# Conditioned four-layer residual stack on one core: VectorE and GpSimd work of the second layer put in another order

## The chip, the cores and the metric

The kernel runs on 1 core of one Trainium2 chip. The metric is the device time of one execution in microseconds; the time before is 3216.46 us, the median of 3 runs (3215.81 to 3218.46).

## The reference, cut to what matters

x is 32 sequences of 128 tokens with 512 features, in float32. Each layer adds its result to x.

```python
def reference(x, cond, mask, ...):
    x = x + layer0(x, cond)            # attention, modulated
    x = x + layer1(x, mask, cond)      # attention, then RMS norm (below)
    x = x + layer2(x, cond)            # x' = x + attention(norm(x)); x' + swiglu(norm(x'))
    x = x + layer3(x, cond)            # quaternion mix
    return x

def layer1(x, mask, cond):
    q, k, v = heads(x @ Wq.T), heads(x @ Wk.T), heads(x @ Wv.T)     # 16 heads of 32
    scores = where(mask, -inf, q @ k.T * 32 ** -0.5)
    out = merge(softmax(scores) @ v) @ Wo.T
    xn = out / sqrt(mean(out * out, -1) + 1e-6) * rms_scale
    shift, sc = split(silu(cond) @ Wc.T + bc, 2)                    # one pair per sequence
    return xn * (1 + sc) + shift
```

## The kernel before, in words

Activations are kept transposed, features on partitions. The 4096 tokens are cut into `G` = 16 groups of two sequences (`T` = 256 tokens, `CH` = 4 chunks of 128 features). A phase `prepare` is followed by `attention` three times, with the tags L0, L1 and L2, and by `gated_mlp`. The profile's names leave the digit out, so all three attentions read `L_...`. The change touches `attention` alone.

float32 products are made of parts: a tile x is split into a high part `xh` (ScalarE's copy to the matmul's rounded type, `high_x`) and a low part `xl` = x - xh (`low_x`), and each product is three matmuls: high by high, low by high, high by low. So are q, k and the output `ot`; probabilities and values are split in the same manner (`pth`/`ptl`; `v1`, `v2`, `v3` with the remainder `vr` on GpSimd: `rest_of_values` makes `vr`, `third_values` writes `v3`, shown as `keep_v`).

The order is written out by hand, in program order for each engine; semaphores join them. One iteration `body(i)` has `SLOTS` = 12 slots. In slots 0 to 7 TensorE makes the scores of units 0 to 7 of group i (a unit is four heads of one sequence) and, one slot later, transposes the unit's exponentials (L625); later slots hold the products with the values. Between these stand pieces of projections: of the output of group i - 1 in slots 0 and 1 (L574 to L576 with `L_oth`), then K, Q and V of group i + 1. For each unit VectorE takes the maximum (`L_top`, L953) and subtracts it (`L_shifted`, L957), ScalarE takes the exponential (L799), TensorE transposes, ScalarE and VectorE read the two parts (`L_pth`, `L_ptl`). Every two units `normalise(i, j)` on VectorE divides a quarter of the attention's result by the sums (L969 to L984), in slots 4, 6, 8 and 9. `turn_output` transposes it, `low_output` (L998) makes its low part in slots 8 and 11; the output projection waits for the last one.

Layer L1 normalises the projected output `af` of group i - 1 within `body(i)`: in slot 4 VectorE copies gain and shift columns (`norm_gains`) and folds the squares (`add_squares`: `L_half`, then `L_quarter`); in slot 6 TensorE sums over partitions (`norm_sum`, L681, which waits for `L_quarter`) and ScalarE takes the root; in slot 7 VectorE takes the reciprocal (`norm_start`); in slot 9 `norm_scale` (L1021) multiplies `af` by it, after the last `normalise`; in slot 11 `norm_add` adds af times gain to `xres` in eight instructions (L1039) and signals `y_ready`, on which SyncE stores the group. `xres` is x, to which GpSimd has added the shift (`shift_residual`, L1196), as soon as `norm_gains` has signalled. GpSimd's `low_x` (L1154) stands at the end of its body (the first group's is made on VectorE, L1054), and TensorE's first K projection and SyncE's next load of x wait for it (`x_split`).

L2 uses the same functions on the next x (`norm_scale`, and `norm_end` with L1029 in place of `norm_add`), and keeps GpSimd's `low_x`.

Of the kernel before, what the change touches and what calls it, by code (L numbers as in the profile page):

```python
# [51 lines left out]
def f32(ap):  # L52
    return ap.bitcast(F32)
# [292 lines left out]
def attention(nc, hold, k, tag, x_in, x_out, wh, wl, weights):  # L346
# [7 lines left out]
    with ExitStack() as ctx:  # L354
# [66 lines left out]
        sq_ready, sum_step = sem("sq_ready"), sem("sum_step")  # L421
        norm_step, eps_set, y_ready, gains_ready = sem("norm_step"), sem("eps_set"), sem("y_ready"), sem("gains_ready")

# [483 lines left out]
        def _(dve):  # L907
# [98 lines left out]
            def norm_gains(n, gains, biases):  # L1006

                if positive(n):
                    dve.wait_ge(y_ready if L1 else x_normed, n)
                nc.vector.tensor_copy(gt[:], gains[:, :, bass.ds(NB * n, NB)])  # L1010
                nc.vector.tensor_copy(bt[:], biases[:, :, bass.ds(NB * n, NB)]).then_inc(gains_ready, 1)

# [9 lines left out]

            def norm_end(n, tile, out_sem):

                dve.wait_ge(norm_step, 2 * n + 2)
                for c in range(CH):
                    for b in range(NB):
                        part = tile[:, c, b * P:(b + 1) * P]
                        last = nc.vector.tensor_scalar(part, part, gt[:, c, b:b + 1], bt[:, c, b:b + 1], ALU.mult, ALU.add)  # L1029
                last.then_inc(out_sem, 1)  # L1030

            def norm_add(n):

                dve.wait_ge(norm_step, 2 * n + 2)
                dve.wait_ge(res_ready, n + 1)
                for c in range(CH):
                    for b in range(NB):
                        o = slice(b * P, (b + 1) * P)
                        last = nc.vector.scalar_tensor_tensor(out=xres[:, c, o], in0=af[:, c, o], scalar=gt[:, c, b:b + 1], in1=xres[:, c, o],  # L1039
                                                              op0=ALU.mult, op1=ALU.add)  # L1040
                last.then_inc(y_ready, 1)

            if L1 or L2:
                nc.vector.memset(eps[:], 1e-6).then_inc(eps_set, 1)
            if L2:
                add_squares(0)
                ws.low(dve, 0)
                norm_gains(0, k["g1"], k["b1"])
                norm_start(0, 0)
                norm_scale(0, xf)  # L1050
                norm_end(0, xf, x_normed)

            dve.wait_ge(x_high, 1)
            nc.vector.tensor_tensor(xl[:], xf[:], f32(xh[:]), ALU.subtract).then_inc(x_split, 1)  # L1054
            if L2:
# [3 lines left out]
            for s in range(SLOTS):  # L1059
                if s == 6 and L2:  # L1060
                    add_squares(1)
                for n in split_after(s):
                    ws.low(dve, n)
                for fill in ended(s):
                    if active(-1, fill):
                        read_fill(0, fill)
                if s == 7 and L2:
                    norm_gains(1, k["g1"], k["b1"])
                    norm_start(1, 1)
                    norm_scale(1, xf)  # L1070
                    norm_end(1, xf, x_normed)

            def body(i):
                first = isinstance(i, int) and i == 0
                for s in range(SLOTS):
# [6 lines left out]
                    for fill in readable(s):  # L1082
                        if active(i, fill):
                            read_fill(group_of(i, fill), fill)
                    if s in (4, 6, 8, 9):
                        normalise(i, (4, 6, 8, 9).index(s))
                    if 1 <= s <= UNITS:
                        low_probs(i, s - 1)
# [32 lines left out]
                    if s == 4 and L2 and has(i, 2):  # L1121
                        norm_gains(i + 2, k["g1"], k["b1"])
                        add_squares(i + 2)
                    if s == 9 and L1 and not first:
                        norm_scale(i - 1, af)
                    if s == 9 and L2 and has(i, 2):
                        norm_scale(i + 2, xf)
                    if s == 7 and L1 and not first:
                        norm_start(i - 1, b_turn(i, "norm"))
                    if s == 7 and L2 and has(i, 2):  # L1130
                        norm_start(i + 2, b_turn(i, "norm"))
                    if s == 11 and L1 and not first:
                        norm_add(i - 1)
                    if s == 11 and L2 and has(i, 2):
                        norm_end(i + 2, xf, x_normed)
                    if s == 7 and L0 and has(i, 1):
# [6 lines left out]
            if L1:  # L1143
                norm_gains(G - 1, k["gain"], k["shift"])
                add_squares(G - 1)
                norm_start(G - 1, 3 * G - 1)
                norm_scale(G - 1, af)
                norm_add(G - 1)

        @block.gpsimd  # L1150
        def _(pool):
# [27 lines left out]
            def body(i):  # L1179
# [4 lines left out]
                if has(i, 1):  # L1184
                    if L0:
                        low_t(i + 1)
                    for b in range(NB):
                        rest_of_values(i + 1, b)
                if has(i, 2):
                    low_x(i + 2)  # L1190

            def shift_residual(n):
                pool.wait_ge(gains_ready, n + 1)
                pool.wait_ge(res_loaded, 16 * (n + 1))
                x4 = xres[:].rearrange("p c (b t) -> p c b t", b=NB)
                nc.gpsimd.tensor_tensor(x4, x4, bt[:].unsqueeze(3).broadcast_to([P, CH, NB, P]), ALU.add).then_inc(res_ready, 1)  # L1196
# [530 lines left out]
```

## Time and profile before

| | |
|---|---|
| median of 3 runs | 3216.46 us |
| profiled execution, its own time | 3217.66 us |
| its span | 3215.6 us |
| mean granted TensorE clock | 0.968 |
| L0 attention / L1 attention / L2 attention / MLP begin at about | 37 / 779 / 1478 / 2100 us |
| busy share: TensorE, VectorE, ScalarE, GpSimd | 94%, 67%, 43%, 20% |

PE is TensorE, DVE is VectorE, ACT is ScalarE, POOL is GpSimd, SPq the queue of SyncE. A name `L_xres<-L_af,L_gt,L_xres` gives the tile that an instruction writes and those that it reads; `L_bank_...` are PSUM banks, all other tiles of these rows lie in SBUF. In a timeline a row with x8 stands for eight instructions in a row, from the start of the first to the end of the last. The idle time before an instruction counts from the modelled end of the one before it.

### The profile page before, as it was taken

To read this page: it belongs to the slowest core of one execution; us is meant where nothing else is said; L and a number is where in the kernel's file an instruction comes from. 1 tells how busy PE (TensorE), PEld (TensorE's weight loads), DVE (VectorE), ACT (ScalarE), POOL (GpSimd) and SP (SyncE) were. 2 spreads that over 40 slices of the span, in tenths; PEclk is the share of its full clock that TensorE was granted. 3 is DMA by queue.
4 is the path that set the end of the run, shared out by engine and by line. 5 is a ranking of instruction groups with operands and counts; after the bars stand their busy time and mean duration, and the time that the engine had idled before them with its cause. 6 is when DMAs were issued, how large, how long until landed. Compare 5 with 4: busy or idle time off the path is not lost. (4 is left out here: it accounts for less than half of the span.)

```text
span 3215.6 us, 67582 instructions
## 1 busy us (share of the span) xinstructions
PE 3015.6 (94%) x25333; PEld 2713.8 (84%) x25333; DVE 2143.1 (67%) x3771; ACT 1373.5 (43%) x2220; POOL 631.7 (20%) x432
## 2 busy tenths in 40 slices
PE   6999999997899999984999999869999999999998
PEld 5999999996888888884999999858888888888886
DVE  5777677775688888885788888664444454556544
ACT  3444444443455555553566566432222233222221
POOL 1112222110122222211111221112222221111111
PEclk8999999998999999996999999979999999999999
DMA  5444344433444444433455555331122132111111
GB/s 164 113 111 108 101 108 107 110 99 114 112 116 117 115 115 117 115 95 115 122 139 136 130 137 133 98 137 53 66 67 77 53 112 72 53 40 39 52 40 40
DMA packets 198921, 317.07 MB, mean 99 GB/s; under 512 B 42112, under 2 KB 99584, under 8 KB 198304
## 3 DMA queue, kind: packets, MB, share of 16 engines
q1 hardware_dynamic: 198816, 315.64, 35.5%
q8 instruction: 70, 1.15, 0.2%
q14 instruction: 35, 0.29, 0.0%
HBM read 122.53 MB, written 41.94 MB: 51 GB/s over the span
## 5 line engine op out<-in xcount | busy, mean ns | idle before, releaser
L1560 DVE TENSOR_TENSOR mlp_act_t<-mlp_bank_u,mlp_sg 128x512 f32<-128x512 f32 x128 | 88.4, 691 | 452.8 <-ACT mlp_sg L1462 449.2
L799 ACT ACTIVATE L_shifted<-L_shifted,keep_lift 128x512 f32<-128x512 f32 x384 | 275.8, 718 | 190.2 <-DVE L_shifted L957 188.0
L1462 ACT ACTIVATE mlp_sg<-mlp_bank_g 128x512 f32<-128x512 f32 x128 | 76.6, 598 | 627.6 <-PE mlp_bank_u L1375 627.4
L1602 POOL TENSOR_TENSOR mlp_al<-mlp_act_t,mlp_ah 128x512 fp32r<-128x512 f32 x128 | 174.8, 1366 | 856.5 <-ACT mlp_ah L1468 856.5
L953 DVE TENSOR_REDUCE L_top<-L_bank_s 128x4 f32<-128x512 f32 x384 | 262.9, 685 | 111.2 <-PE L_bank_s L616 109.4
L794 ACT ACTIVATE L_pth<-L_bank_t 128x512 f16<-128x512 f32 x384 | 227.7, 593 | 228.3 <-PE L_bank_t L625 227.9
L961 DVE TENSOR_TENSOR L_ptl<-L_bank_t,L_pth 128x512 f16<-128x512 f32 x384 | 262.2, 683 | 79.8 <-ACT L_pth L794 79.0
L1161 POOL TENSOR_TENSOR L_vr<-L_vf,keep_v 128x512 f32<-128x512 f32 x96 | 122.0, 1272 | 884.7 <-ACT keep_v L829 884.7
L625 PE MATMUL L_bank_t<-keep_pack,L_shifted 128*128 128x128 f32 x1536 | 251.9, 288 | 43.3 <-ACT L_shifted L799 43.0
L957 DVE TENSOR_TENSOR L_shifted<-L_bank_s,L_top 128x512 f32<-128x512 f32 x384 | 265.5, 691 | 18.4 <-DVE L_top L953 3.3
L574 PE MATMUL L_bank_a<-L_xh,L_wkh 128*128 128x256 f32 x768 | 231.9, 302 | 38.3 <-DVE L_wkl L102 24.3
L616 PEld LDWEIGHTS L_bank_s<-L_ks,L_qs 96*128 96x128 f32 x1536 | 222.0, 196 | 20.0 <-issue 6.8
L641 PE MATMUL L_bank_o<-keep_v,L_pth 128*128 128x34 bf16 x4608 | 232.8, 179 | 5.3 <-DVE L_of L984 5.2
L574 PE MATMUL L_bank_a<-L_oth,L_woh 128*128 128x256 f32 x768 | 230.1, 300 | 4.5 <-DVE L_otl L998 4.5
L616 PE MATMUL L_bank_s<-L_ks,L_qs 96*128 96x128 f32 x1536 | 226.0, 271 | 8.4 <-DMA L_qs<-L_qh 8.4
L574 PE MATMUL L_bank_a<-L_xh,L_wqh 128*128 128x256 f32 x768 | 231.5, 301 | 0.0
L575 PE MATMUL L_bank_a<-L_xh,L_wkl 128*128 128x256 f32 x768 | 221.1, 288 | 0.0
L576 PE MATMUL L_bank_a<-L_xl,L_wkh 128*128 128x256 f32 x768 | 220.8, 288 | 0.0
L576 PE MATMUL L_bank_a<-L_otl,L_woh 128*128 128x256 f32 x768 | 220.6, 287 | 0.0
L575 PE MATMUL L_bank_a<-L_oth,L_wol 128*128 128x256 f32 x768 | 220.5, 287 | 0.0
L1373 PE MATMUL mlp_bank_g<-mlp_hh,mlp_wgh 128*128 128x512 f32 x512 | 207.7, 406 | 12.6 <-POOL mlp_hl L1592 12.6
L641 PE MATMUL L_bank_o<-keep_v,L_ptl 128*128 128x34 bf16 x3072 | 219.0, 178 | 0.0
(266 smaller groups left out, 8825.7 us busy)
## 6 DMA issues: line engine op xcount, KB each, us to landing
L_ks<-L_kh SPq DMA_DIRECT2D x768, 64.0 KB, 2.0
L_qs<-L_qh SPq DMA_DIRECT2D x768, 64.0 KB, 2.0
L_ks<-L_kl SPq DMA_DIRECT2D x384, 64.0 KB, 2.0
L_qs<-L_ql SPq DMA_DIRECT2D x384, 64.0 KB, 2.0
resid<-L_xres SPq DMA_DIRECT2D x48, 512.0 KB, 2.8
L_xf<-resid SPq DMA_DIRECT2D x32, 512.0 KB, 3.8
L_xres<-resid SPq DMA_DIRECT2D x32, 512.0 KB, 4.1
mlp_xf<-resid SPq DMA_DIRECT2D x32, 512.0 KB, 4.6
```

What stands on the lines that cost most here:

```text
L574: nc.tensor.matmul(out, w_h, x_h, start=first, stop=False)
L575: nc.tensor.matmul(out, w_l, x_h, start=False, stop=False)
L576: return nc.tensor.matmul(out, w_h, x_l, start=False, stop=last)
L616: mm = nc.tensor.matmul(bank_s[u % 2][:, h * P:(h + 1) * P], q_h, k_h, start=not L1, stop=not L1 or h == 3)
L625: mm = nc.tensor.transpose(bank_t[u % 2][:, h * P:(h + 1) * P], shifted[:, u % 2, h, :], k["ident"][:])
L641: mm = nc.tensor.matmul(bank_o[:, o:o + VW], p[:, u % 2, h, :], v[:, b, 4 * c + h, :], start=(n == 0), stop=(n == len(passes) - 1))
L794: nc.scalar.activation(pth[:, u % 2], bank_t[u % 2][:].rearrange("p (h j) -> p h j", h=4), ACT.Copy).then_inc(p_high, 1)
L799: nc.scalar.activation(shifted[:, u % 2], shifted[:, u % 2], ACT.Exp, bias=k["lift"][:, 0:1], scale=SCALE).then_inc(exp_done, 1)
L953: nc.vector.reduce_max(top[:, u % 2, :], src, AX_X).then_inc(top_ready, 1)
L957: nc.vector.tensor_tensor(shifted[:, u % 2], src, bcast_last(top[:, u % 2, :], P), ALU.subtract).then_inc(shift_done, 1)
L961: nc.vector.tensor_tensor(ptl[:, u % 2], bank_t[u % 2][:].rearrange("p (h j) -> p h j", h=4), pth[:, u % 2], ALU.subtract).then_inc(p_low, 1)
L1373: nc.tensor.matmul(out, w[0], x_h, start=first, stop=False)
```

## The change: what it does

1. L1's `low_x` moves from GpSimd's end of `body(i - 1)` to VectorE's slot 1 of `body(i)`, between `L_shifted` and `L_ptl`; groups 0 and 1 are done as before.
2. `norm_scale` of slot 9 is issued ahead of the last `normalise`, for L1 and L2.
3. `norm_add` (L1) and `norm_end` (L2) are cut in halves of four instructions, one in slot 10 and one in slot 11 behind `low_output`.
4. `shift_residual` waits for `sum_step`, which `L_quarter` signals, in place of `gains_ready`, which goes away.

```diff
-            def norm_add(n):
-                dve.wait_ge(norm_step, 2 * n + 2)
-                dve.wait_ge(res_ready, n + 1)
-                for c in range(CH):
+            def norm_add(n, m):
+                if m == 0:
+                    dve.wait_ge(norm_step, 2 * n + 2)
+                    dve.wait_ge(res_ready, n + 1)
+                for c in (2 * m, 2 * m + 1):
                     for b in range(NB):
...
-                last.then_inc(y_ready, 1)
+                if m == 1:
+                    last.then_inc(y_ready, 1)
+
+            def low_x(n):
+                dve.wait_ge(x_high, n + 1)
+                nc.vector.tensor_tensor(xl[:], xf[:], f32(xh[:]), ALU.subtract).then_inc(x_split, 1)
...
+                    if s == 9 and L1 and not first:
+                        norm_scale(i - 1, af)
+                    if s == 9 and L2 and has(i, 2):
+                        norm_scale(i + 2, xf)
                     if s in (4, 6, 8, 9):
                         normalise(i, (4, 6, 8, 9).index(s))
+                    if s == 1 and L1 and not first and has(i, 1):
+                        low_x(i + 1)
                     if 1 <= s <= UNITS:
                         low_probs(i, s - 1)
...
-                    if s == 9 and L1 and not first:
-                        norm_scale(i - 1, af)
-                    if s == 9 and L2 and has(i, 2):
-                        norm_scale(i + 2, xf)
...
-                    if s == 11 and L1 and not first:
-                        norm_add(i - 1)
-                    if s == 11 and L2 and has(i, 2):
-                        norm_end(i + 2, xf, x_normed)
+                    if s >= 10 and L1 and not first:
+                        norm_add(i - 1, s - 10)
+                    if s >= 10 and L2 and has(i, 2):
+                        norm_end(i + 2, xf, s - 10)
...
-                if has(i, 2):
+                if has(i, 2) and not L1:
                     low_x(i + 2)
...
-                pool.wait_ge(gains_ready, n + 1)
+                pool.wait_ge(sum_step, 2 * (n + 1))
                 pool.wait_ge(res_loaded, 16 * (n + 1))
```

`norm_end` is cut in the same way as `norm_add`. In the rows below, lines 1021, 953 to 998 keep their numbers; L1039 becomes L1042, L1154 of L1 becomes L1049 on VectorE, L1196 becomes L1208, L1161 becomes L1173 and L1165 becomes L1177.

VectorE in L1, from the end of slot 8 of an iteration into the next one's slots 0 and 1 (the last but one iteration, written out in full); before:

```order
L961 TENSOR_TENSOR L_ptl<-L_bank_t,L_pth 128x512
L969 RECIPROCAL L_rz<-L_bank_o 128x8
L976 TENSOR_SCALAR L_rz<-L_rz,keep_any_key 128x8
L984 TENSOR_TENSOR L_of<-L_bank_o,L_rz 128x2x128
L1021 TENSOR_TENSOR L_af<-L_af,L_rs 128x1024
L998 TENSOR_TENSOR L_otl<-L_bank_b,L_oth 128x512
L1039 SCALAR_TENSOR_TENSOR L_xres<-L_af,L_gt,L_xres 128x128 x8
L953 TENSOR_REDUCE L_top<-L_bank_s 128x4
```

And with the change:

```order
L961 TENSOR_TENSOR L_ptl<-L_bank_t,L_pth 128x512
L1021 TENSOR_TENSOR L_af<-L_af,L_rs 128x1024
L969 RECIPROCAL L_rz<-L_bank_o 128x8
L976 TENSOR_SCALAR L_rz<-L_rz,keep_any_key 128x8
L984 TENSOR_TENSOR L_of<-L_bank_o,L_rz 128x2x128
L1042 SCALAR_TENSOR_TENSOR L_xres<-L_af,L_gt,L_xres 128x128 x4
L998 TENSOR_TENSOR L_otl<-L_bank_b,L_oth 128x512
L1042 SCALAR_TENSOR_TENSOR L_xres<-L_af,L_gt,L_xres 128x128 x4
L953 TENSOR_REDUCE L_top<-L_bank_s 128x4
```

The scaling stands ahead of the last L969, and the adds are four and four around L998.

VectorE in L1, slots 0 and 1 at the start of that iteration; before:

```order
L953 TENSOR_REDUCE L_top<-L_bank_s 128x4
L957 TENSOR_TENSOR L_shifted<-L_bank_s,L_top 128x512
L953 TENSOR_REDUCE L_top<-L_bank_s 128x4
L957 TENSOR_TENSOR L_shifted<-L_bank_s,L_top 128x512
L961 TENSOR_TENSOR L_ptl<-L_bank_t,L_pth 128x512
L953 TENSOR_REDUCE L_top<-L_bank_s 128x4
```

And with the change:

```order
L953 TENSOR_REDUCE L_top<-L_bank_s 128x4
L957 TENSOR_TENSOR L_shifted<-L_bank_s,L_top 128x512
L953 TENSOR_REDUCE L_top<-L_bank_s 128x4
L957 TENSOR_TENSOR L_shifted<-L_bank_s,L_top 128x512
L1049 TENSOR_TENSOR L_xl<-L_xf,L_xh 128x1024
L961 TENSOR_TENSOR L_ptl<-L_bank_t,L_pth 128x512
```

L1049, the low part of x, has come in between the second L957 and L961.

GpSimd in the loop body of L1; before:

```order
L1165 TENSOR_TENSOR keep_v<-L_vr,keep_v 128x16x32
L1164 REGISTER_ALU
L1165 TENSOR_TENSOR keep_v<-L_vr,keep_v 128x16x32
L1194 REGISTER_ALU
L1196 TENSOR_TENSOR L_xres<-L_xres,L_bt 128x1024
L1160 ISA
L1161 TENSOR_TENSOR L_vr<-L_vf,keep_v 128x512
L1160 REGISTER_ALU
L1161 TENSOR_TENSOR L_vr<-L_vf,keep_v 128x512
L1153 REGISTER_ALU
L1154 TENSOR_TENSOR L_xl<-L_xf,L_xh 128x1024
```

And with the change:

```order
L1177 TENSOR_TENSOR keep_v<-L_vr,keep_v 128x16x32
L1176 REGISTER_ALU
L1177 TENSOR_TENSOR keep_v<-L_vr,keep_v 128x16x32
L1206 REGISTER_ALU
L1208 TENSOR_TENSOR L_xres<-L_xres,L_bt 128x1024
L1172 ISA
L1173 TENSOR_TENSOR L_vr<-L_vf,keep_v 128x512
L1172 REGISTER_ALU
L1173 TENSOR_TENSOR L_vr<-L_vf,keep_v 128x512
```

L1154 is gone from the end of the body; the residual shift keeps its place and has another semaphore to wait for.

## Rows read from the trace of the kernel before

**Rows 1.** The page, busy time: us, share of the span, instructions.

```profile
PE 3015.6 (94%) x25333; PEld 2713.8 (84%) x25333; DVE 2143.1 (67%) x3771; ACT 1373.5 (43%) x2220; POOL 631.7 (20%) x432
```

**Rows 2.** Stretches: us, busy (instructions) of each engine, granted clock (PEclk), DMA share, GB/s.

```profile
core 0: us, PE busy (x) PEld busy (x) DVE busy (x) ACT busy (x) POOL busy (x), PEclk, DMA share, GB/s
890.10:930.60 40.50, 37.81 (x413) 35.61 (x412) 33.95 (x57) 22.46 (x36) 9.14 (x7) 1.00 0.45 118
930.60:972.60 42.00, 39.32 (x412) 37.08 (x412) 34.00 (x57) 22.59 (x36) 9.08 (x7) 0.96 0.44 112
1059.70:1063.80 4.10, 4.02 (x21) 3.92 (x21) 1.29 (x2) 3.18 (x7) 2.21 (x2) 0.58 0.52 123
```

**Rows 3.** Waits, 860 to 1470 us: who, for whom, us in total, times, longest us.

```profile
ACT L_shifted L799 <- DVE L_shifted L957: 107.6, 43, 4.7
...
PE L_bank_t L625 <- ACT L_shifted L799: 31.2, 29, 2.0
...
PE L_bank_b L681 <- DVE L_quarter L1004: 12.4, 16, 3.8
```

**Rows 4.** Timeline of TensorE: start, us, instruction [idle before, releaser].

```profile
start us, us, engine line op out<-in xcount [idle before <-releaser]
...
1097.67 0.56 PE L616 MATMUL L_bank_s<-L_ks,L_qs 96*128 96x128 f32 x4
...
1099.44 0.28 PE L576 MATMUL L_bank_a<-L_otl,L_woh 128*128 128x256 f32 x1
1101.75 0.66 PE L625 MATMUL L_bank_t<-keep_pack,L_shifted 128*128 128x128 f32 x4 [2.04 <-ACT L_shifted L799]
...
1103.69 0.40 PE L612 MATMUL L_bank_s<-keep_mask,keep_ident_r 128*128 128x512 f32 x1
1103.92 0.56 PE L616 MATMUL L_bank_s<-L_ks,L_qs 96*128 96x128 f32 x4
...
1104.70 0.37 PE L574 MATMUL L_bank_a<-L_xh,L_wkh 128*128 128x256 f32 x1
```

**Rows 5.** Timeline of VectorE, same columns.

```profile
1090.80 0.21 DVE L969 RECIPROCAL L_rz<-L_bank_o 128x8 f32<-128x8 f32 x1 [1.25 <-PE L_bank_o L641]
...
1091.65 2.06 DVE L1021 TENSOR_TENSOR L_af<-L_af,L_rs 128x1024 f32<-128x1024 f32 x1
...
1094.23 5.19 DVE L1039 SCALAR_TENSOR_TENSOR L_xres<-L_af,L_gt,L_xres 128x128 f32<-128x128 f32 x8
1099.34 0.68 DVE L953 TENSOR_REDUCE L_top<-L_bank_s 128x4 f32<-128x512 f32 x1
```

**Rows 6.** Timeline of GpSimd, same columns.

```profile
1091.51 1.12 POOL L1161 TENSOR_TENSOR L_vr<-L_vf,keep_v 128x512 f32<-128x512 f32 x1 [14.98 <-ACT keep_v L829]
1095.42 1.19 POOL L1161 TENSOR_TENSOR L_vr<-L_vf,keep_v 128x512 f32<-128x512 f32 x1 [2.79 <-ACT keep_v L829]
1096.57 2.44 POOL L1154 TENSOR_TENSOR L_xl<-L_xf,L_xh 128x1024 fp32r<-128x1024 f32 x1
1102.30 2.21 POOL L1165 TENSOR_TENSOR keep_v<-L_vr,keep_v 128x512 bf16<-128x512 f32 x2 [3.29 <-ACT keep_v L833]
```

**Rows 7.** Instructions of one line: count, duration ns min/median/max, first and last start.

```profile
L1039 DVE SCALAR_TENSOR_TENSOR L_xres<-L_af,L_gt,L_xres x128: 334/341/2476, 888.9 to 1474.3; 128x128 f32<-128x128 f32 x128
...
L1004 DVE TENSOR_TENSOR L_quarter<-L_half x32: 424/426/2004, 869.5 to 2003.6; 128x256 f32<-128x256 f32 x32
...
L1021 DVE TENSOR_TENSOR L_af<-L_af,L_rs x16: 1214/2059/2064, 886.3 to 1471.2; 128x1024 f32<-128x1024 f32 x16
...
L1054 DVE TENSOR_TENSOR L_xl<-L_xf,L_xh x3: 1225/1225/1226, 42.2 to 1493.4; 128x1024 fp32r<-128x1024 f32 x3
...
L961 DVE TENSOR_TENSOR L_ptl<-L_bank_t,L_pth x370: 677/681/694, 100.1 to 2050.0; 128x512 f16<-128x512 f32 x185
```

**Rows 8.** Timeline of TensorE around the norm's sum.

```profile
1117.42 0.67 PE L681 MATMUL L_bank_b<-L_quarter,keep_ones 128*128 128x256 f32 x2 [0.46 <-DVE L_quarter L1004]
...
1119.41 0.66 PE L625 MATMUL L_bank_t<-keep_pack,L_shifted 128*128 128x128 f32 x4 [0.18 <-ACT L_shifted L799]
```

**Rows 9.** Timeline of GpSimd in the third layer, two iterations.

```profile
1813.10 2.40 POOL L1154 TENSOR_TENSOR L_xl<-L_xf,L_xh 128x1024 fp32r<-128x1024 f32 x1 [1.52 <-ACT L_xh L839]
...
1848.48 2.40 POOL L1154 TENSOR_TENSOR L_xl<-L_xf,L_xh 128x1024 fp32r<-128x1024 f32 x1 [1.52 <-ACT L_xh L839]
```

More of the change, by code:

```diff
@@ L421, in attention @@
         sq_ready, sum_step = sem("sq_ready"), sem("sum_step")
-        norm_step, eps_set, y_ready, gains_ready = sem("norm_step"), sem("eps_set"), sem("y_ready"), sem("gains_ready")
+        norm_step, eps_set, y_ready = sem("norm_step"), sem("eps_set"), sem("y_ready")
         fills = [("o", 0), ("o", 1), ("k", 0), ("q", 0), ("k", 1), ("q", 1)] + ([("c", 0), ("c", 1)] if L0 else []) + [("v", 0), ("v", 1)]
@@ L1010, in norm_gains @@
                 nc.vector.tensor_copy(gt[:], gains[:, :, bass.ds(NB * n, NB)])
-                nc.vector.tensor_copy(bt[:], biases[:, :, bass.ds(NB * n, NB)]).then_inc(gains_ready, 1)
+                nc.vector.tensor_copy(bt[:], biases[:, :, bass.ds(NB * n, NB)])
             def norm_start(n, turn):
@@ L1021, in norm_scale, with norm_end @@
                 nc.vector.tensor_tensor(tile[:], tile[:], bcast_mid(rs[:], CH), ALU.mult).then_inc(norm_step, 1)
-            def norm_end(n, tile, out_sem):
-                dve.wait_ge(norm_step, 2 * n + 2)
-                for c in range(CH):
+            def norm_end(n, tile, m):
+                if m == 0:
+                    dve.wait_ge(norm_step, 2 * n + 2)
+                for c in (2 * m, 2 * m + 1):
                     for b in range(NB):
@@ L1029, in norm_end @@
                         last = nc.vector.tensor_scalar(part, part, gt[:, c, b:b + 1], bt[:, c, b:b + 1], ALU.mult, ALU.add)
-                last.then_inc(out_sem, 1)
-            def norm_add(n):
-                dve.wait_ge(norm_step, 2 * n + 2)
-                dve.wait_ge(res_ready, n + 1)
-                for c in range(CH):
+                if m == 1:
+                    last.then_inc(x_normed, 1)
+            def norm_add(n, m):
+                if m == 0:
+                    dve.wait_ge(norm_step, 2 * n + 2)
+                    dve.wait_ge(res_ready, n + 1)
+                for c in (2 * m, 2 * m + 1):
                     for b in range(NB):
@@ L1040, in norm_add @@
                                                               op0=ALU.mult, op1=ALU.add)
-                last.then_inc(y_ready, 1)
+                if m == 1:
+                    last.then_inc(y_ready, 1)
+            def low_x(n):
+                dve.wait_ge(x_high, n + 1)
+                nc.vector.tensor_tensor(xl[:], xf[:], f32(xh[:]), ALU.subtract).then_inc(x_split, 1)
             if L1 or L2:
@@ L1050, in _ @@
                 norm_scale(0, xf)
-                norm_end(0, xf, x_normed)
-            dve.wait_ge(x_high, 1)
-            nc.vector.tensor_tensor(xl[:], xf[:], f32(xh[:]), ALU.subtract).then_inc(x_split, 1)
+                for m in range(2):
+                    norm_end(0, xf, m)
+            low_x(0)
             if L2:
@@ L1070, in _ @@
                     norm_scale(1, xf)
-                    norm_end(1, xf, x_normed)
+                    for m in range(2):
+                        norm_end(1, xf, m)
             def body(i):
@@ L1147, in _ @@
                 norm_scale(G - 1, af)
-                norm_add(G - 1)
+                for m in range(2):
+                    norm_add(G - 1, m)
         @block.gpsimd
```

## The prediction

> **What bounds the kernel now.** I read the busy table first: TensorE is busy 94% of the span and no other engine over 67% [rows 1], so the change can pay only where it lets TensorE stand less. The second layer (about 780 to 1478 us) is where all moved instructions run. Cut into its loop iterations, one takes 40.50 us with TensorE busy 37.81; four of the thirteen between 890 and 1422 us take 42.00 at a mean granted clock of 0.96 [rows 2]. The waits of that stretch name two releasers on TensorE: ScalarE's exponential `L_shifted`, which itself waits for VectorE, and `L_quarter` on VectorE, which the norm's sum needs [rows 3].
>
> The timelines show how. TensorE issues its last matmul of a piece at 1099.44 and the transposes of unit 0 only at 1101.75; matmuls follow each other at about 0.12, so 2.19 us are lost from start to start, of which the profile counts 2.04 as idle since it models a matmul's end [rows 4]. Those transposes want the exponential of unit 0, which wants `L_top` and `L_shifted`, and VectorE begins `L_top` at 1099.34, straight behind eight residual adds that took 5.19 us [rows 5]. Its scores had long been there. Beside these adds GpSimd runs `L_vr` and then the low part of x, 1095.42 to 1099.01 [rows 6]. An add takes 0.34 by itself and up to 2.48; `L_quarter` takes 0.43 or 2.00; the scaling 1.21 or 2.06 [rows 7]. So a VectorE instruction whose operands all lie in SBUF stands until GpSimd's current one ends, 2.1 + 0.9 us in the adds, 0.85 in the scaling, 1.57 in `L_quarter` (there the holder is the residual shift). Instructions that read PSUM do not: 370 `L_ptl` subtractions range only from 677 to 694 ns, and in that range are those with GpSimd at work beside them [rows 7].
>
> **The change part by part.**
>
> *Scaling before the last normalisation.* VectorE stands 1.25 us before that normalisation [rows 5], and GpSimd is free until 1091.51 [rows 6]. The scaling then costs 1.22, not 2.06, from about 1089.55 to 1090.8, just as the normalisation's input arrives at 1090.80. Cost 0, saving 2.06 on VectorE behind it. The cover is exactly as wide as the instruction; if it slips, `L_of` and the transposes behind it slip by that.
>
> *Four adds in slot 10, four in slot 11.* The first four start at 1091.65 and are held by `L_vr` to 1092.63, ending near 1093.6; the low output follows at about 1093.5, when today the scaling is just over (1091.65 + 2.06) [rows 5, 6]. The second four need 1.1 us (5.19 less the holds of 3.0, over eight, is 0.27 each) and end near 1095.2, before `L_vr` at 1095.42. So `L_top` starts near 1095.2 in place of 1099.34. From `L_top` to the transposes the chain takes 1101.75 - 1099.34 = 2.41, so they could start at 1097.6; TensorE wants them at 1099.56. The stall of 2.19 goes whole, with 2 us in hand.
>
> *Low part of x to VectorE, slot 1.* It is removed from GpSimd (2.44) and costs VectorE 1.23 [rows 6, 7], in 14 iterations. With everything 2.2 us earlier, it starts near 1099.7 (after the second `L_shifted`, whose scores end at 1098.2 [rows 4]), where VectorE would otherwise wait for unit 0's transposes. GpSimd's two `keep_v` subtractions (2.21) would then run from about 1098.1 to 1100.3, so it may be held 0.6 and ends near 1101.5. TensorE now starts the next K projection, which needs it, 2.95 after the transposes [rows 4]; that will be at 1102.5. One microsecond in hand: cost 0. Behind it on VectorE stands `L_ptl` of unit 0, wanted by TensorE only three slots on. On SyncE the next load of x waits for it too, but it is queued behind the store and the last stack of Q copies, which start when the adds end (now 4 us sooner), and nobody wants that x for an iteration: cost 0.
>
> *Residual shift after `L_quarter`.* `L_quarter` is 1.57 earlier. TensorE's norm sum stands 0.46 for it by the profile and the transposes behind 0.18 [rows 8]; from start to start each is 0.16 more, as above: 0.62 and 0.34. Together they are under 1.57 and both go: 0.96 in each of 14 iterations. The shift (2.19) now lies beside `L_top`, `L_shifted`, `L_ql` and `L_ptl`, all with a PSUM operand, 2.4 us of work that isn't held; nobody wants the shift before slot 10.
>
> *The clock.* In four iterations the granted clock is 0.58 for about 4 us straight after the 2.04 us stall [rows 2], between the two levels of 1.2 and 2.4 GHz. That costs 42.00 - 40.50 = 1.50 each. Nothing else in such an iteration differs, and without a stall I expect no fall.
>
> *Third layer.* Its scaling and final multiply-adds are reordered in the same way, but one iteration there takes 35.38 us (1813.10 to 1848.48) [rows 9] and TensorE shows no idle in the waits of its steady part: 0. It also gives a check. The second layer's iteration is that one plus 8 mask matmuls of 0.23 (start to start [rows 4]), so without stalls it should take 35.38 + 1.84 = 37.2. The sum here says 40.46 - 2.19 - 0.96 = 37.3.
>
> *Ends of the layer.* The waits for `L_quarter` come to 12.4 in 16 times; 14 of 0.46 leave 6.0 for the last two, longest 3.8 [rows 3]. Each is in a stretch without filler matmuls and loses up to the 1.57 (the very last about 1.0, where the instruction ahead is held, too). The step into the last iteration has a smaller copy of the main stall, about 1. Together I take 4, bounds 2 and 6.
>
> The sum: 13 x 2.19 = 28.5 (the stall follows iterations 1 to 13), 14 x 0.96 = 13.4, 4 x 1.5 = 6.0, and 4.0, together 51.9. Counting only what the profile calls idle it is 13 x 2.04 + 14 x 0.64 + 6 + 4 = 45.5; I take the first since the third layer's iteration agrees with it. The profiled execution took 3217.66 (span 3215.6), 1.2 above the median of 3216.46: 3217.7 - 51.9 = 3165.8, or about **3165** on the median's scale.
>
> **Where the Trainium skill says otherwise.** What rows 6 and 7 show is that one low part costs GpSimd 2.44 and holds VectorE most of that, and costs VectorE 1.23 when it does it itself. The Trainium skill (Perfetto Trace Analysis, Optimizing Scalar/DVE Operations) warns that, as the two engines share a port, shifting work between them might not help. Taken strictly, a hold would only change its place; then just the shift of the residual and the clock would pay, and the first rival below is what comes out. The rows speak against it here, because the adds are moved off GpSimd's instructions as well.
>
> **The rivals.**
>
> *A smaller stall stays or a new one opens.* For it: VectorE's queue is in strict order, and three fits are narrow (the scaling in 1.25 us, the low output at 1093.5, the low part of x with 1 us in hand). If the low part is held behind both `keep_v` subtractions starting later than I place them, it ends up to 1.2 later than needed. About 1 us in each of 13 iterations gives 3165 + 13 = 3178, and if the clock still falls 3184. Against: each fit is computed from rows and none depends on another engine being faster. By the Trainium skill (SBUF — State Buffer, Who interferes with whom) whichever of the two starts first keeps the pair for its whole instruction, so the low part could hold `keep_v` too; no row of the second layer shows this order.
>
> *The stalls go, the clock falls stay.* They come every third iteration with an even period, which could be a beat of its own. Then 3165 + 6 = 3171.
>
> *The change moves nothing.* If the exponential were late for ScalarE's reasons, the stall would stay: 3216. Against: what releases it is VectorE, 107.6 us in 43 waits [rows 3].
>
> *Slower.* VectorE now carries the wait for the high part of x inside its chain. Everything behind that wait, unit 0's `L_ptl` and the scores of unit 2, would stand, and TensorE's K projection with them. It decides from the point at which the low part ends after 1102.5; for a net loss it must cost over 3.15 us in each iteration, thus end after 1105.7, over 4 us later than worked out. At 1105.7 plus 1 us in 14 iterations: 3216 + 14 = 3230. Against: ScalarE makes that high part an iteration's end ahead of slot 0, where GpSimd could use it at 1096.57 [rows 6].
>
> **How the numbers follow.** 0.66 for the forecast, whose own range is 3160 to 3172 (the ends at 2 or 6, stalls counted by either measure); 0.15 for a remaining stall (3172 to 3184); 0.11 for the clock; 0.05 for no movement; 0.03 for slower. The range 3158 to 3184 takes in the first three. A measurement of this kernel tells about 0.2%, 6.4 us, from no change. Faster by more: 0.92; within: 0.05; slower by more: 0.03.
>
> **What would show it.** In the profile after: second-layer iterations of about 37.3 us with no clock under 1.00; no wait of `L_bank_t` for `L_shifted` of 2 us and none of `L_bank_b` for `L_quarter` but the last ones; eight adds in two groups with at most one add of over 1 us; `L_quarter` at 0.43 and the scaling at 1.21 throughout; the low part of x on VectorE at 1.2 to 1.9. A new releaser `L_xl` on a K matmul, or iterations above 38.5, would show me wrong.

## Result and profile after

The change takes 3164.27 us in the median against 3217.46 for the kernel before in the same comparison: 0.983 of its time, 95% interval 0.981 to 0.985, so about 53 us faster. (One of the four executions was disturbed and lasted 8826.65 us; it is left out of the ratio, and the median of the other three is 3163.57.) The forecast was 3165. The profiled execution took 3162.08 us with a span of 3160.1, where before's took 3217.66 with 3215.6: 55.6 us less.

The page after, busy time of each engine:

```profile
PE 3006.0 (95%) x25333; PEld 2710.6 (86%) x25333; DVE 2105.0 (67%) x3785; ACT 1376.1 (44%) x2220; POOL 579.7 (18%) x418
```

TensorE's share rises from 94 [rows 1] to 95%; GpSimd's falls from 20 to 18%. Two stretches of the second layer after, in the columns of rows 2: nearly its whole steady part, and one iteration.

```profile
880.00:1340.00 460.00, 460.00 (x5068) 438.46 (x5067) 385.62 (x709) 280.55 (x435) 80.75 (x64) 1.00 0.49 127
908.70:945.80 37.10, 37.10 (x412) 35.41 (x411) 31.14 (x58) 22.68 (x35) 6.35 (x6) 1.00 0.49 127
```

TensorE is busy throughout and the granted clock is 1.00; over 880 to 1340 us it was 430.59 busy and 0.99 in the kernel before. From one start of the norm's sum (L681) to the next every iteration now takes 37.12 us, where it took about 40.46, four times about 42.0 and the last time 40.14. The 13 iterations took 531.7 us before (871.62 to 1403.36) and take 482.6 (871.59 to 1354.15): 49.2 less. The end of the layer, from the last of these sums to the first one of the third layer, goes from 81.11 to 77.30, 3.8 less. Over that last stretch the mean granted clock was 0.78 before and is 0.81, so its 3.8 us aren't all waits. Together that is 53.0 of the 55.5 us of span. The other 2.5 lie in the third layer and the MLP (1731.1 to 1728.6), where the runs of this study differ by as much among themselves (1734.2 in `e4_no_lowx_move` below), so I give them to nothing.

The waits after between 860 and 1380 us, which answer to rows 3:

```profile
DVE L_top L953 <- PE L_bank_s L616: 54.9, 58, 1.7
...
ACT L_shifted L799 <- DVE L_shifted L957: 29.7, 42, 1.2
```

In this window no row has TensorE's matmuls as the ones that wait for another engine. In the kernel before, over the same 860 to 1380 us, they wait 26.8 us for `L_shifted` and 5.9 for `L_quarter`, ScalarE waits 94.1 for VectorE at `L_shifted` (now 29.7), and VectorE 28.0 for TensorE at `L_top` (now 54.9): VectorE now waits for TensorE more than TensorE for it. The waits at the layer's end, after 1380 us, stay (below).

VectorE's timeline after, one iteration from slot 9 into the next slot 1, answering to rows 5:

```profile
1068.72 1.22 DVE L1021 TENSOR_TENSOR L_af<-L_af,L_rs 128x1024 f32<-128x1024 f32 x1
1070.56 0.21 DVE L969 RECIPROCAL L_rz<-L_bank_o 128x8 f32<-128x8 f32 x1 [0.63 <-PE L_bank_o L641]
...
1071.41 1.91 DVE L1042 SCALAR_TENSOR_TENSOR L_xres<-L_af,L_gt,L_xres 128x128 f32<-128x128 f32 x4
1073.25 0.68 DVE L998 TENSOR_TENSOR L_otl<-L_bank_b,L_oth 128x512 fp32r<-128x512 f32 x1
1073.85 1.13 DVE L1042 SCALAR_TENSOR_TENSOR L_xres<-L_af,L_gt,L_xres 128x128 f32<-128x128 f32 x4
1074.90 0.68 DVE L953 TENSOR_REDUCE L_top<-L_bank_s 128x4 f32<-128x512 f32 x1
...
1078.03 0.69 DVE L953 TENSOR_REDUCE L_top<-L_bank_s 128x4 f32<-128x512 f32 x1 [1.53 <-PE L_bank_s L616]
...
1079.36 1.79 DVE L1049 TENSOR_TENSOR L_xl<-L_xf,L_xh 128x1024 fp32r<-128x1024 f32 x1
1081.07 0.68 DVE L961 TENSOR_TENSOR L_ptl<-L_bank_t,L_pth 128x512 f16<-128x512 f32 x1
```

GpSimd's beside it, answering to rows 6:

```profile
1071.27 1.12 POOL L1173 TENSOR_TENSOR L_vr<-L_vf,keep_v 128x512 f32<-128x512 f32 x1 [13.13 <-ACT keep_v L829]
1075.19 1.13 POOL L1173 TENSOR_TENSOR L_vr<-L_vf,keep_v 128x512 f32<-128x512 f32 x1 [2.79 <-ACT keep_v L829]
1077.86 2.21 POOL L1177 TENSOR_TENSOR keep_v<-L_vr,keep_v 128x512 bf16<-128x512 f32 x2 [1.54 <-ACT keep_v L833]
```

The scaling stands 0.63 us ahead of its normalisation's input (1070.56) and is not held (1.22). Of the first four adds one is held by `L_vr`, as 1.91 against 1.13 for the second four shows, and the second four end at 1074.98, before the next `L_vr` at 1075.19. `L_top` follows at once, 4.42 us ahead of unit 0's transposes (1079.32), where the chain needs 2.41 [rows 4, 5], and VectorE then waits 1.53 for TensorE's scores of unit 1. The low part of x (1079.36) is held until about the end of `keep_v` (1080.07) and ends at 1081.15. TensorE's timeline at the two places where it stood or could stand, answering to rows 4:

```profile
1079.20 0.28 PE L576 MATMUL L_bank_a<-L_otl,L_woh 128*128 128x256 f32 x1
1079.32 0.60 PE L625 MATMUL L_bank_t<-keep_pack,L_shifted 128*128 128x128 f32 x4
...
1082.20 0.36 PE L574 MATMUL L_bank_a<-L_xh,L_wkh 128*128 128x256 f32 x1
...
1082.53 0.29 PE L576 MATMUL L_bank_a<-L_xl,L_wkh 128*128 128x256 f32 x1
```

The transposes follow the last matmul by 0.12 (before, 2.31), and the first matmul that needs the low part of x (L576 on `L_xl`) starts at 1082.53, the projection at 1082.20, 1.05 after it is there.

The durations by line, as in rows 7:

```profile
L1042 DVE SCALAR_TENSOR_TENSOR L_xres<-L_af,L_gt,L_xres x128: 333/340/1126, 885.8 to 1421.4; 128x128 f32<-128x128 f32 x128
...
L1208 POOL TENSOR_TENSOR L_xres<-L_xres,L_bt x16: 1894/1897/1897, 870.6 to 1415.0; 128x1024 f32<-128x1024 f32 x16
...
L1004 DVE TENSOR_TENSOR L_quarter<-L_half x32: 424/425/427, 870.1 to 1948.1; 128x256 f32<-128x256 f32 x32
...
L1021 DVE TENSOR_TENSOR L_af<-L_af,L_rs x16: 1212/1215/1224, 883.1 to 1418.3; 128x1024 f32<-128x1024 f32 x16
...
L1049 DVE TENSOR_TENSOR L_xl<-L_xf,L_xh x17: 1224/1783/1804, 41.9 to 1440.1; 128x1024 fp32r<-128x1024 f32 x17
```

`L_quarter` is 0.42 throughout (before, up to 2.00), the scaling 1.21 to 1.22 (2.06), the longest add 1.13 (2.48). L1208 in the group is the residual shift. The low part has two prices, 1.22 alone and 1.78 to 1.80 beside `keep_v`.

### The profile page after: what moved, and what is told of

Read it like the earlier page. It is cut to its first block and busy times, and to the rows that moved or that the text cites. A ratio compares the mean times of both kernels' runs of the same rounds, so it can differ in the third digit from the quotient of the medians.

```text
span 3160.1 us, 67582 instructions
## 1 busy us (share of the span) xinstructions
PE 3006.0 (95%) x25333; PEld 2710.6 (86%) x25333; DVE 2105.0 (67%) x3785; ACT 1376.1 (44%) x2220; POOL 579.7 (18%) x418
## 3 DMA queue, kind: packets, MB, share of 16 engines
q8 instruction: 69, 1.13, 0.2%
## 5 line engine op out<-in xcount | busy, mean ns | idle before, releaser
L961 DVE TENSOR_TENSOR L_ptl<-L_bank_t,L_pth 128x512 f16<-128x512 f32 x384 | 261.8, 682 | 49.0 <-ACT L_pth L794 48.9
L957 DVE TENSOR_TENSOR L_shifted<-L_bank_s,L_top 128x512 f32<-128x512 f32 x384 | 265.4, 691 | 18.3 <-DVE L_top L953 3.3
L1173 POOL TENSOR_TENSOR L_vr<-L_vf,keep_v 128x512 f32<-128x512 f32 x96 | 108.9, 1135 | 888.4 <-ACT keep_v L829 888.4
L576 PE MATMUL L_bank_a<-L_xl,L_wkh 128*128 128x256 f32 x768 | 221.1, 288 | 0.0
L1385 PE MATMUL mlp_bank_g<-mlp_hh,mlp_wgh 128*128 128x512 f32 x512 | 207.5, 405 | 12.6 <-POOL mlp_hl L1604 12.6
L576 PE MATMUL L_bank_a<-L_otl,L_woh 128*128 128x256 f32 x768 | 219.0, 285 | 0.0
```

Of the source, the lines that this page charges most:

```text
L576: return nc.tensor.matmul(out, w_h, x_l, start=False, stop=last)
L957: nc.vector.tensor_tensor(shifted[:, u % 2], src, bcast_last(top[:, u % 2, :], P), ALU.subtract).then_inc(shift_done, 1)
L961: nc.vector.tensor_tensor(ptl[:, u % 2], bank_t[u % 2][:].rearrange("p (h j) -> p h j", h=4), pth[:, u % 2], ALU.subtract).then_inc(p_low, 1)
L1385: nc.tensor.matmul(out, w[0], x_h, start=first, stop=False)
```

## Experiments

In the table an iteration is the distance of two starts of the norm's sum in the second layer, and "stall" the longest idle time of TensorE ahead of unit 0's transposes. A "fall" is an iteration with the granted clock down behind that stall; in the kernel before, `e1_shift_only` and `e9_fill7` it makes the iteration about 1.5 us longer, in `e10_fill10` up to 2.7. Iterations, stalls and falls are those of one profiled execution per kernel. Each ratio is against runs of the kernel before on the same chip; their medians lie between 3217.4 and 3218.6 us.

| kernel | median us | ratio to before (95%) | iteration us | stall us | falls of 13 |
|---|---|---|---|---|---|
| before | 3217.46 | | 40.46 | 2.04 | 4 |
| the change | 3164.27 | 0.9832 (0.9813 to 0.9851) | 37.12 | none | 0 |
| `e1_shift_only` | 3213.90 | 0.9985 (0.9976 to 0.9995) | 40.90 (with fall) | 2.04 | 13 |
| `e2_lowx_only` | 3183.05 | 0.9887 (0.9871 to 0.9904) | 38.31 | none | 0 |
| `e3_split_only` | 3180.78 | 0.9883 (0.9867 to 0.9900) | 38.20 | none | 0 |
| `e6_lowx_order_only` | 3183.85 | 0.9897 (0.9881 to 0.9914) | 38.33 | none | 0 |
| `e4_no_lowx_move` | 3165.97 | 0.9836 (0.9819 to 0.9852) | 37.12 | none | 0 |
| `e5_lowx_and_shift` | 3166.04 | 0.9844 (0.9827 to 0.9860) | 37.24 | none | 0 |
| `e11_scale_first_unsplit` | 3161.93 | 0.9827 (0.9811 to 0.9843) | 37.12 | none | 0 |
| `e7_fill2` | 3163.63, one run | | 37.12 | none | 0 |
| `e8_fill6` | 3183.57, one run | | 38.72 | 1.39 | 0 |
| `e9_fill7` | 3206.16, one run | | 39.31, with fall 40.88 | 1.98 | 8 |
| `e10_fill10` | 3240.97, one run | | 41.1 to 43.8 | 3.77 | 12 |

**The residual shift alone.** The kernel before, and only

```diff
-                pool.wait_ge(gains_ready, n + 1)
+                pool.wait_ge(sum_step, 2 * (n + 1))
```

> The kernel before, with the residual shift alone waiting for L_quarter's signal. Theory (three separate holds, each with its own stall): L_quarter falls from 2.00 to 0.43 us, the norm sum's 0.46 and the 0.18 behind it go, 0.96 us in each of 14 iterations and about 2.5 at the layer's end; the 2.04 us stall of slot 1 and its four clock falls stay. About 3201. Rival (the holds are one chain, and time won at the norm sum is given back at slot 1): 3215 or more, with the slot 1 stall at 3 us.

This missed: 4.7 us (0.15%) in place of some 17. `L_quarter` is at 0.42 to 0.43 and TensorE no longer waits for it. But the stall ahead of the transposes is as it was, and the clock now falls behind every one of them in the profiled execution. Less the 1.5 us of a fall an iteration would take 39.4, 1.1 less than before (0.96 was forecast); that is an estimate, since none of them is without a fall. TensorE's waits for them (880 to 1340 us), and one iteration and the 4 us behind a stall:

```profile
PE L_bank_t L625 <- ACT L_shifted L799: 22.4, 11, 2.1
```

```profile
871.40:912.30 40.90, 38.85 (x412) 36.91 (x411) 32.51 (x57) 22.68 (x35) 8.79 (x7) 0.96 0.45 116
1101.00:1105.00 4.00, 4.00 (x23) 3.90 (x23) 1.23 (x2) 3.32 (x6) 1.96 (x2) 0.58 0.47 106
```

The iteration takes 40.90 at 0.96, the stretch behind the stall runs at 0.58, as in the four iterations of rows 2. 13 x 1.08 = 14.0 us were saved (1.08 is the step from `e3_split_only` to `e4_no_lowx_move` below) and nine more falls at about 1.53 took 13.8 of them back: the 13 iterations take 531.5 us against 531.7. The ten executions range from 3209.8 to 3216.6, and the profiled one is the longest. If falls alone make the difference, the median execution (2.7 less) had about two fewer and the shortest (6.8 less) four or five fewer; that is an estimate, as their iterations weren't seen.

**The low part of x alone.** The kernel before, with `low_x` on VectorE in slot 1 and not on GpSimd:

```diff
+                    if s == 1 and L1 and not first and has(i, 1):
+                        low_x(i + 1)
...
-                if has(i, 2):
+                if has(i, 2) and not L1:
```

> The kernel before, with the low part of x alone moved to VectorE's slot 1. Theory: the eight adds lose the hold of 2.1 us but keep the one by L_vr (about 3.05 in all), L_top starts 2.1 us sooner, the 2.04 stall shrinks to under 0.15 and the clock falls go; the norm sum's stalls stay. 28 + 6: about 3182. Rival (the low part costs VectorE as much as its hold did): 3205 or more.

As expected, to 1 us. What TensorE still waits for (880 to 1340 us):

```profile
PE L_bank_b L681 <- DVE L_quarter L1004: 5.5, 12, 0.5
...
PE L_bank_t L625 <- ACT L_shifted L799: 2.2, 12, 0.2
```

and the adds:

```profile
L1039 DVE SCALAR_TENSOR_TENSOR L_xres<-L_af,L_gt,L_xres x128: 334/336/1216, 890.3 to 1441.8; 128x128 f32<-128x128 f32 x128
```

With the low part gone the longest add is 1.22: the hold of 2.1 us goes and that of `L_vr` (0.9) stays. That is enough for the stall ahead of unit 0's transposes: no idle time is left there, and from start to start 0.12 us. Both waits that remain belong to the norm's sum and to the transposes right behind it [rows 8]; `L_quarter` is as late as before.

**The scaling first and the adds in halves alone.** The change, with the low part left on GpSimd and the shift waiting for `gains_ready`.

> The change without its move of the low part (it stays on GpSimd) and without the later residual shift: only the scaling ahead of the last normalisation and the adds in halves. Theory that the move and the split cure the same stall: the second four adds are over before GpSimd begins the low part, nothing is held by it, the stall of slot 1 goes whole and with it the clock falls: 3181 to 3183. Rival (the low part must leave GpSimd): it still holds an add or the first L_top, 3205 or more.

3180.78, iterations of 38.20: the same stall goes by another way, with the same two waits at the norm's sum left on TensorE (5.5 and 2.2 us in all). The move on one side and the scaling with the halves on the other are substitutes, since they remove one stall. No run has the scaling first, or the halves, by itself beside GpSimd's low part, so which of the two cures it here is open.

**The change without the move of the low part.**

> The change with the low part of x left on GpSimd. Theory that the move adds nothing once the adds are early: 3164, within 3 us of the change, and second-layer iterations of 37.1 us. Rival (the move carries part of the gain): each iteration 1 to 2 us longer, 3178 to 3195.

3165.97 against 3164.27, both with iterations of 37.12: the move adds nothing to the other parts. The stretch in the columns of rows 2:

```profile
880.00:1340.00 460.00, 460.00 (x5052) 438.46 (x5051) 365.01 (x695) 280.39 (x433) 111.00 (x77) 1.00 0.49 128
```

TensorE is as busy as with the change, VectorE has 20.6 us less to do and GpSimd 30.3 more.

**The low part and the shift together, scaling and adds as before.**

> The kernel before with the low part of x on VectorE and the residual shift later, but the scaling and the eight adds where they were. Theory (the move and the split are two cures of one stall, the shift cures the other): iterations of 37.2 to 37.4 us, no clock falls, about 3167. Rival (all three parts are needed): iterations of 38 or more, 3177 or more.

3166.04, iterations of 37.24, no wait on TensorE. The scaling is still held to 2.06 and the eight adds take 3.05 together, and an iteration is 0.12 longer than with the change, all of it at unit 0's transposes from start to start, where the profile shows no idle time.

**The hold by itself.** If the stall comes from GpSimd's low part standing beside the adds, then it must go with no work moved or removed, only with that instruction held back on GpSimd until the adds are done:

```diff
                 if has(i, 2):
+                    if L1 and positive(i):
+                        pool.wait_ge(y_ready, i)
                     low_x(i + 2)
```

> The kernel before, where GpSimd's low part of x in the loop of the second layer waits for the end of the adds (y_ready). Nothing changes engine, place or size. Theory (a VectorE instruction with all operands in SBUF stands while GpSimd runs): the longest add falls from 2.48 to about 1.2, L_top comes 2.1 us sooner, iterations of 38.3 as with the low part on VectorE, 3183. Rival (it is VectorE's queue or GpSimd's speed as such): the stall of slot 1 stays near 2.04, iterations of 40.5 or longer, since GpSimd's work is only later.

It does: 3183.85, 38.33 in an iteration. GpSimd and VectorE in that kernel:

```profile
1079.35 1.12 POOL L1161 TENSOR_TENSOR L_vr<-L_vf,keep_v 128x512 f32<-128x512 f32 x1 [14.97 <-ACT keep_v L829]
1083.27 1.19 POOL L1161 TENSOR_TENSOR L_vr<-L_vf,keep_v 128x512 f32<-128x512 f32 x1 [2.80 <-ACT keep_v L829]
1085.29 2.38 POOL L1154 TENSOR_TENSOR L_xl<-L_xf,L_xh 128x1024 fp32r<-128x1024 f32 x1 [0.83 <-DVE L_xres L1039]
```

```profile
1079.49 2.06 DVE L1021 TENSOR_TENSOR L_af<-L_af,L_rs 128x1024 f32<-128x1024 f32 x1
...
1082.07 3.06 DVE L1039 SCALAR_TENSOR_TENSOR L_xres<-L_af,L_gt,L_xres 128x128 f32<-128x128 f32 x8
```

The low part starts at 1085.29, 0.2 after the last add; the eight adds take 3.06 in place of 5.19, one of them held by the `L_vr` of 1083.27. Both engines do just what they did before; one instruction starts 0.83 us after the end of `L_vr` in place of at once, and that is worth 33 us.

**The adds not cut.** The change with all eight adds in slot 11, the scaling still first:

```diff
-                    if s >= 10 and L1 and not first:
-                        norm_add(i - 1, s - 10)
+                    if s == 11 and L1 and not first:
+                        for m in range(2):
+                            norm_add(i - 1, m)
```

> The change with all eight adds in slot 11 behind the low output; scaling ahead of the last normalisation, low part on VectorE and the later shift stay. Theory (any one way of ending the adds a microsecond ahead is enough): no stall over 0.1 us in an iteration, 37.1 to 37.2, no clock fall, 3164 to 3167. Rival (the halves matter): a stall of L_bank_t for L_shifted of 0.5 us or more, 3171 or more.

3161.93, and the intervals of the two ratios overlap: cutting them brings nothing that can be told.

**How much is in hand.** The change with N maxima over `L_half` into a scratch tile at the end of slot 11, each 0.61 us of VectorE work that nobody needs:

```diff
+                    if s == 11 and L1 and not first and has(i, 1):
+                        for m in range(N):
+                            nc.vector.reduce_max(scr[:, 2 * m:2 * m + 2], half[:], AX_X)
```

> The change, with two more maxima over L_half on VectorE (0.60 us apart, result unused) at the end of slot 11 in the second layer. Theory (VectorE has 2.0 us in hand there): iterations stay at 37.12, time within 3 us of the change. Rival (VectorE has become the bound): each iteration 1.2 longer, 3180.

> The change, with six such maxima (3.6 us). Theory: 2.0 are hidden, the stall before unit 0's transposes is back with 1.5 to 1.7 us, iterations of 38.7, plus clock falls of 1.4 to 1.5 us in some or in all of them, as the shift alone showed (40.1 where it falls): 3185 without, 3205 with a fall in each. Rival (the falls need the longer stall of 2.04): iterations of 38.7 throughout.

> The change with seven maxima at the end of slot 11: the stall before unit 0's transposes should be 2.0 us, as long as in the kernel before, at an iteration of 39.3 without a clock fall. If the length of the stall decides on the fall, falls of 1.4 to 1.5 us come back in a third of the iterations or in more: 3197 to 3212. If its place in time decides as well, their number differs from before (a third) and from the shift alone (each), and may be none: 3191.

> The change with ten maxima (6.0 us): the stall should be 3.8 us, iterations of 41.1. Longer than any stall in the loop before, so if a longer stall makes a fall surer, there is one in nearly every iteration: 42.6 on average and 3236; without falls 3216.

Two of them (1.2 us) are free: 3163.63, and TensorE waits for nothing from 880 to 1340 us. Six last 3.64 and make an iteration 1.60 longer, so 2.0 us were in hand, as the prediction said; seven give the same 2.0 by an iteration without a fall (4.24 - 2.19 = 2.05). TensorE's waits from 880 to 1340 us with six, seven and ten:

```profile
PE L_bank_t L626 <- ACT L_shifted L800: 16.7, 12, 1.4
```

```profile
PE L_bank_t L626 <- ACT L_shifted L800: 23.8, 12, 2.0
```

```profile
PE L_bank_t L626 <- ACT L_shifted L800: 41.4, 11, 3.8
```

These also separate stall and clock. Stalls of 1.4 us cause no fall, and 13 x 1.60 = 20.8 accounts for the loss: the span is 21.4 longer than the change's and 19.8 longer than with two maxima. With 1.98 the clock falls in 8 of 13 iterations and the stretch's mean is 0.97:

```profile
880.00:1340.00 460.00, 436.21 (x4640) 413.61 (x4639) 396.58 (x734) 256.72 (x398) 84.70 (x58) 0.97 0.45 118
```

One more maximum (0.61) thus cost 22.6 us, of which 13 x 0.59 = 7.7 are the stall and 8 x 1.57 = 12.6 the clock; the other 2.3 lie outside these iterations. Each of these kernels ran once. Ten maxima give a stall of 3.77, falls in 12 of 13 iterations and 3240.97 us, 5 more than expected: the mean iteration is 42.87 (expected 42.6), as six of the falls cost 2.2 to 2.7 us and not 1.5.

The six maxima stand beside a `L_vr` of GpSimd, and this row and the two timelines bear on who is held (the first is VectorE's, the last GpSimd's):

```profile
L1150 DVE TENSOR_REDUCE L_scr<-L_half x84: 664/671/675, 889.5 to 1395.7; 128x2 f32<-128x512 f32 x84
```

```profile
1121.83 3.64 DVE L1150 TENSOR_REDUCE L_scr<-L_half 128x2 f32<-128x512 f32 x6
```

```profile
1122.12 1.13 POOL L1177 TENSOR_TENSOR L_vr<-L_vf,keep_v 128x512 f32<-128x512 f32 x1 [2.80 <-ACT keep_v L830]
```

Neither is: 664 to 675 ns in 84 instructions, 3.64 / 6 = 0.61 from start to start, and `L_vr` takes its 1.13.

## Why the prediction was right, and where not

**The bound and its chain.** Right: TensorE stood for VectorE, and VectorE for GpSimd. `e6_lowx_order_only` shows the last link by itself.

**Scaling before the last normalisation.** Cost 0, as said; there were 0.6 us of room where the prediction left none, as the scaling began at 1068.72, 1.84 ahead of the normalisation's input. It was not run alone.

**Four adds and four.** The times fit: one add held, the second four over before `L_vr`. But the step gave the stall of 2.19 to these adds and the low part of x jointly, and this is where the prediction's account was thinnest. Each of three edits removes it alone: the low part's move (iteration 2.15 shorter), scaling and halves (2.26), or a mere wait on GpSimd (2.13). With the low part moved the halves aren't needed (`e11_scale_first_unsplit`); without that move they were not tried apart from the scaling. The forecast of the sum doesn't depend on the split, and so came out right.

**Low part of x.** It takes 1.79 with 0.57 of hold (forecast 0.6) and ends at 1081.15, 1.05 ahead of the projection (forecast 1.0). Cost 0 was right; its gain is 0 too, given the other parts (`e4_no_lowx_move`). The remark that shifting work between VectorE and GpSimd might not help, which the Trainium skill makes (Perfetto Trace Analysis, Optimizing Scalar/DVE Operations), is thus borne out in `e4_no_lowx_move` and not in `e2_lowx_only`, which moves the same instruction and gains 1.1%. The instruction was to be kept from lying beside the adds; which engine does it was secondary.

**Residual shift.** 0.96 in an iteration was forecast. Where the clock is full, 1.07 was measured (38.31 to 37.24, from `e2_lowx_only` to `e5_lowx_and_shift`) and 1.08 (38.20 to 37.12, from `e3_split_only` to `e4_no_lowx_move`): the 0.62 and 0.34 of the working, and 0.13 in the matmuls behind them. As a share of the kernel's time it is not a term of its own: with the stall still there it bought 4.7 us, and on top of `e2_lowx_only` or `e3_split_only` 17.0 and 14.8. The prediction added 13.4 for it and 6.0 for the clock as if each stood alone; my expectation for `e1_shift_only` shows what that led to.

**The sum of an iteration.** Forecast 3.15 without the clock, measured 40.46 - 37.12 = 3.34. Start-to-start losses of 2.20, 0.62 and 0.33 at the three places agree with the 2.19, 0.62 and 0.34 of the working; another 0.2 in all came back in the first few matmuls behind each restart, which ran slower. That is 2.5 us in 13 iterations. The check against the third layer (37.2) was nearer than the sum (37.3).

**The clock.** The four falls are gone: 6.0 forecast and 6.1 measured: the 13 iterations give 49.2 = 13 x 3.34 + 4 x 1.53 - 0.3, the last because the thirteenth took only 40.14 before. The rival by which the falls have a beat of their own is refuted by nine kernels that have none in 13 iterations each, and by `e9_fill7`, where they come back with the stall. "Without a stall no fall" held. It is not the stall's length alone, though: 2.04 us gave 4 falls of 13 in the kernel before and 13 of 13 in `e1_shift_only`. They differ in the idle times at the norm's sum that the first has and the second hasn't, and so in when the stalls come. These counts are of one execution each, and what decides was not tried.

**Ends of the layer and third layer.** 4.0 us were forecast for the ends and 0.96 for the fourteenth iteration, which lies in the same stretch; 3.8 were measured for both, so this term was 1.2 too high, and some of the 3.8 may be the clock's (0.78 to 0.81). TensorE's waits there, 1354 to 1431 us:

```profile
PE L_bank_b L681 <- DVE L_quarter L1004: 3.3, 2, 3.1
...
PE L_bank_t L625 <- ACT L_shifted L799: 2.3, 3, 1.4
```

The longest wait for `L_quarter` is 3.1 and was 3.8 [rows 3]. One iteration of the third layer takes 35.31 us in place of 35.38 [rows 9]: nothing, as said.

**The other rivals.** No smaller stall opened: none of the three narrow fits slipped. The slower one needed the low part of x to end over 4 us later than worked out; it ended where it was put.

So the mechanism and the total (forecast 51.9 us off the profiled execution, measured 55.6) stand; of the difference of 3.7, the 13 iterations gave 2.2 more than the 47.0 that the working puts in them, the end of the layer 1.2 less than its 4.0 and 0.96, and the later layers 2.5 that no run here attributes. That the total fits to 4 us is helped by luck: one of the three errors has the other sign.

## What to carry to other kernels

When an instruction has one duration at some times and another at others, look at what the neighbouring engine runs in that moment before counting operations: here a one-line wait on GpSimd, with no work moved, gave 33 of the change's 53 us. Test the parts of a change one at a time and in pairs, for cures of the same stall don't add up (33 to 38 us for any one, by the ratios, and none for the second), and a part can look worthless only because a stall elsewhere eats it (4.7 us alone, 15 to 17 us after another part). Fill a gap with dummy work to learn how much is in hand: here 2.0 us in an iteration are free, the next 1.6 cost about 20 us, and 0.6 more cost 23, since they bring the falls of the clock with them (one run of each).

## What the runs showed that I had not expected

**Not every instruction on SBUF tiles is held.** The prediction's sentence that a VectorE instruction stands "whose operands all lie in SBUF" is too wide. The maxima over `L_half` read and write SBUF alone and run beside `L_vr` in 0.61 us, neither held nor holding. Those that were held in the second layer were the adds, the scaling, the low part, `L_quarter` and at the layer's end `L_half`, all with two tile inputs in SBUF. By the Trainium skill (SBUF — State Buffer, Who interferes with whom) a VectorE operation with two SBUF inputs contends with GpSimd's reads, and a plain reduction never does; the row of `L_scr` agrees. Two tile inputs aren't the condition either, though. The multiply-add of the third layer reads one tile and two columns, and its longest took 1.15 us in place of 0.34, beside a `L_vr`:

```profile
L1030 DVE TENSOR_SCALAR L_xf<-L_xf,L_gt,L_bt x128: 333/339/1153, 1436.8 to 1966.5; 128x128 f32<-128x128 f32 x128
```

**The hold goes the other way as well.** The prediction says that no row of the second layer shows VectorE first and GpSimd held. The trace before has one: the residual shift begins at 1074.35, 0.26 after VectorE's `L_half`, and takes 2.19, where it takes 1.90 with the change, behind `L_quarter`. It is plainer in `e5_lowx_and_shift`, where the low part begins first: it takes its 1.22, and the two `keep_v` subtractions take 3.18 in place of 2.21, the longest single one 2.09 in place of 1.12 (the first row is VectorE's, the second GpSimd's).

```profile
1115.97 1.22 DVE L1045 TENSOR_TENSOR L_xl<-L_xf,L_xh 128x1024 fp32r<-128x1024 f32 x1
```

```profile
1116.08 3.18 POOL L1171 TENSOR_TENSOR keep_v<-L_vr,keep_v 128x512 bf16<-128x512 f32 x2 [3.56 <-ACT keep_v L833]
```

So in that kernel the moved low part holds GpSimd, and from 880 to 1340 us no engine has a wait for GpSimd in the profile.

**Falls of the clock come in a share of the stalls that one can't read off their length.** Stalls of 1.4 us: 0 of 13; 1.98: 8; 2.04: 4 in one kernel and 13 in another; 3.8: 12, each count from one execution. A fall costs about 1.5 us (1.51 to 1.57), and behind the stall of 3.8 up to 2.7. What of the stall's place in time, or of the work around it, decides between 4 and 13 stays open.
